# Last layer of a four-layer graph network: its own-quarter blocks in five units of eight block pairs instead of six, and another order of units, products and strip loads

## What is computed

```python
def _L3_gnn_ref(x, adj, weight, bias):
    c = CURV
    deg = jnp.maximum(adj.sum(axis=1, keepdims=True), 1e-08)
    w = adj / deg
    log_ij = _logmap(x[:, None, :], x[None, :, :], c)
    agg = jnp.einsum('ij,ijc->ic', w, log_ij)
    transformed = agg @ weight + bias
    origin = jnp.zeros_like(transformed)
    return _expmap(origin, transformed, c)
...
x = _layernorm(x + _L0_gnn_ref(x, adj, L0_gnn_weight), axis=-1)
x = _layernorm(x + _L1_gnn_ref(x, adj, adj, *L1_weights), axis=-1)
x = _layernorm(x + _L2_gnn_ref(x, adj, L2_gnn_weight, L2_gnn_bias), axis=-1)
x = _layernorm(x + _L3_gnn_ref(x, adj, L3_gnn_weight, L3_gnn_bias), axis=-1)
```

## Time and profile before

| | us |
|---|---|
| Median of 3 runs (1467.49 to 1471.48) | 1470.44 |
| The profiled execution's own time | 1471.95 |
| Its span on the core, first to last instruction | 1470.2 |
| Mean granted TensorE clock of the span | 0.958 |
| Busy over the span: PE / DVE / ACT | 1326.9 / 1204.6 / 982.9 |
| The 72 units' sums (L2888), first to last start | 1051.6 to 1428.7 |

### The profile page before, as it was taken

The page is one execution under the profiler, slowest core; times in us unless marked ns, Lnnn a source line. Parts: engine busy times, 40 slices in busy tenths (PEclk is TensorE's granted clock), DMA queues, the critical chain, the costliest instruction groups (busy, mean ns, idle before and its releaser), DMA issues. The chain is left out here.

```text
span 1470.2 us, 18414 instructions
## 1 busy us (share of the span) xinstructions
PE 1326.9 (90%) x6849; PEld 593.1 (40%) x6874; DVE 1204.6 (82%) x1554; ACT 982.9 (67%) x919; POOL 221.7 (15%) x150
## 2 busy tenths in 40 slices
PE   5899999999898999999999999979987888888893
PEld 1233335334334444444544554434433433334342
DVE  5898978995887888868878977648688898899997
ACT  0001444893673778567676768767789899999985
POOL 1000000000000000000000001242134444444550
PEclk9999999999998999999999999999879999999995
DMA  9999979998999556453554542234533666546610
GB/s 362 409 409 409 374 265 413 409 382 330 415 409 413 185 194 208 178 188 137 191 171 152 193 147 97 90 126 139 205 115 117 213 166 221 184 161 218 219 50 29
DMA packets 134560, 341.56 MB, mean 232 GB/s; under 512 B 7876, under 2 KB 57480, under 8 KB 134280
## 3 DMA queue, kind: packets, MB, share of 16 engines
q1 hardware_dynamic: 118240, 320.88, 59.9%
q10 hardware_dynamic: 16232, 19.51, 3.9%
HBM read 321.49 MB, written 17.83 MB: 231 GB/s over the span
## 5 line engine op out<-in xcount | busy, mean ns | idle before, releaser
L1105 PE MATMUL ps<-ring,X 128*64 128x512 f32 x512 | 235.7, 609 | 7.8 <-DVE ring L2477 7.8
L1106 PE MATMUL ps<-work,X 128*64 128x512 f32 x512 | 235.7, 609 | 0.0
L861 POOL TENSOR_TENSOR ring<-ring,work 128x1024 f32<-128x1024 f32 x72 | 170.1, 2363 | 223.7 <-DVE work L2873 223.7
L1706 ACT ACTIVATE work<-ring 128x2048 f32<-128x2048 f32 x64 | 122.4, 1913 | 89.3 <-PE ps L1121 33.4
L838 POOL TENSOR_SCALAR work<-ring 128x1024 int16<-128x1024 uint8 x24 | 27.4, 1142 | 958.2 <-DMA ring<-codes 884.2
L968 PE MATMUL ps<-ring,work 128*64 128x512 f32 x704 | 160.1, 602 | 1.5 <-DVE Y L2129 1.5
L2477 DVE TENSOR_SCALAR ring<-ring 128x2048 f32<-128x2048 f32 x64 | 78.4, 1225 | 70.4 <-ACT work L1706 70.1
L1105 PEld LDWEIGHTS ps<-ring,X 128*64 128x64 f32 x512 | 67.6, 139 | 146.4 <-issue 139.3
L2151 DVE TENSOR_TENSOR work<-work,ring 128x1024 f32<-128x1024 f32 (+1 forms) x92 | 105.0, 1141 | 4.3 <-DMA ring<-in_adjT 2.4
L1285 PE MATMUL ps<-work 64*128 64x512 f32 x288 | 88.6, 694 | 17.4 <-DVE work L2888 16.0
L1451 ACT ACTIVATE turn_in<-ps 128x512 f32<-128x512 f32 x12 | 7.2, 596 | 144.3 <-PE ps L968 143.4
(11 more groups left out here) (387 smaller groups left out, 2704.0 us busy)
## 6 DMA issues: line engine op xcount, KB each, us to landing
ring<-in_adjT SPq DMA_DIRECT2D x86, 2048.0 KB, 13.6
work<-in_adjT SPq DMA_DIRECT2D x26, 2048.0 KB, 23.1
ring<-in_adjT SPq DMA_DIRECT2D x24, 1024.0 KB, 9.1
ring<-in_adjT SPq DMA_DIRECT2D x48, 512.0 KB, 4.0
ring<-codes SPq DMA_DIRECT2D x32, 512.0 KB, 3.7
ring<-in_adjT SPq DMA_DIRECT2D x64, 256.0 KB, 3.2
codes<-work ACTq DMA_DIRECT2D x32, 256.0 KB, 6.1
codes<-work ACTq DMA_DIRECT2D x64, 128.0 KB, 3.0
```

What stands on the lines that cost most here:

```text
L861: nc.gpsimd.tensor_tensor(u.edges[:, cols], u.edges[:, cols], u.angle[:, cols], ALU.mult).then_inc(weighted, 1)
L1105: nc.tensor.matmul(ps[0:F, h, :], rows, ring[:, r, 2 * (m % 2) + i, cols], start=start, stop=stop)
L1106: mm = nc.tensor.matmul(ps[F:P, h, :], rows, negs[:, m % 2, i, cols], start=start, stop=stop)
L1706: nc.scalar.activation(negs[:, pair], ring[:, r, 2 * pair:2 * pair + 2, :], ACT.Relu, scale=-1.0).then_inc(negs_made, 1)
```

## The change

1. **Five units for a quarter's own pairs.** A new kind **X** (`inner`) takes, in one turned unit, the pairs from blocks 0, 1 to 4, 5 and from 2, 3 to 6, 7. D is now four row blocks against two blocks each, and two of them do for a quarter; the two I stay. Per quarter 2 D + 2 I + 1 X = 5 units (before 4 D + 2 I). In all 48 O, 8 D, 8 I, 4 X = 68 units, of which 60 are turned.
2. **D and X by pieces** (`split`): four edge loads of 256 columns instead of two of 512, four `distances` products of 256 columns instead of two of 512, likewise in `push_apart`. `gather` keeps its four products of 256 columns.
3. **X is a group by itself**: 20 groups instead of 16. Its strip is 0.5 MB (four loads), its sum has 4 sources with one product of 256 columns each, and its `add_mirror` is two operations of 64x256 (a plain copy and one or two memsets where a part has no sum yet).
4. **The planner**: the first group's products go to slots 5 and 6 (before 12 and 13), with a wait for the copied signs, and `turn_sides(2)` now waits for that group's sum. Four sources a slot are also used where a later group would else have to wait (`soon`). Full slots are now 5, 6, 12, 13, 28, 29, 49, 50, 51, 64 and 65; slot 67 has eight sources.
5. **Strips ahead of edges**: the strip's turn stands at `quad_ends[q - 2]`.
6. **The order**: `ORDERS` as in the diff. Groups start at slots 0, 5, 10, 12, 14, 16, 18, 22, 26, 28, 30, 35, 39, 43, 47, 49, 50, 54, 58, 62. In the third string the X stands behind two groups of four O.

```diff
-        ORDERS = [(1, "OOODOODODOODII"), (0, "DDIIDD"), (2, "OOOOOOOODIDIOOOODOOOOD"), (3, "OOOOOOOODIDIOOOOOOOOOOOOOOOODD")]
+        ORDERS = [(1, "OOOODOOOODIIX"), (0, "DIIXD"), (2, "OOOOOOOOXDIIOOOODOOOO"), (3, "OOOOOOOOIIXOOOOOOOOOOOOOOOODD")]
         UNITS = sum(len(order) for I, order in ORDERS)
 
         class Unit:
 
             def __init__(self, n, kind, J, I, k):
                 self.n, self.kind, self.J, self.I = n, kind, J, I
-                self.off, self.turned = kind == "O", kind != "D"
+                self.off, self.turned, self.inner = kind == "O", kind != "D", kind == "X"
+                self.split = kind in "DX"
...
+                elif kind == "X":
+                    self.blocks, self.places = tuple(one[0:2] for one in SETS), (1, 1)
+                    self.seats = (0, GB - 1)
+                    self.sources = [I * CB + c for one in SETS for c in one[2:4]]
                 else:
-                    self.blocks, self.targets = (SETS[0][k], SETS[1][k]), (0, 1)
-                self.rows = tuple(J * CB + b for b in self.blocks)
+                    self.blocks, self.places = tuple((one[k], one[2 + k]) for one in SETS), (0, 1)
+                if not self.split:
+                    self.rows = tuple(J * CB + b for b in self.blocks)
+                self.loads = 1 if self.off else 4 if self.split else 2
...
+            def pieces(self, h):
+
+                return [(b, slice(s * 2 * P, (s + 1) * 2 * P), slice((2 * t + h) * 2 * P, (2 * t + h + 1) * 2 * P))
+                        for s, (b, t) in enumerate(zip(self.blocks[h], self.places))]
...
-            n = max(n, end + (2 if late else 3), LAST_AT + 4)
+            n = max(n, end + (2 if late or not quad else 3), LAST_AT + 4 if quad else 0)
             left = list(range(len(units[end].sources)))
+            soon = quad < 2 or late or n + len(left) // 2 > quad_opens[quad + 2] + 2
             while left:
-                room = len(left) if end == quad_ends[-1] else 4 if quad < 2 or late else 2
+                room = len(left) if end == quad_ends[-1] else 4 if soon else 2
...
-            turns += [(quad_ends[q - 2] + 1, 1, q) for q in range(2, len(quad_ends))]
+            turns += [(quad_ends[q - 2], 1, q) for q in range(2, len(quad_ends))]
...
+                    pe.wait_ge(mirror_added, 1)
...
+                if u.split:
+                    for h in range(2):
+                        for b, at, cols in u.pieces(h):
+                            b += u.J * CB
+                            sp.dma_start(u.edges[:, h * HALF + at.start:h * HALF + at.stop],
+                                         adj_slots[:, b // GB, b % GB, u.I, cols]).then_inc(edges_in[u.row], 16)
+                    return
...
-                    else:
+                    if quad == 0:
+                        pe.wait_ge(signs_copied, SIDED[2])
+                    if quad == 1:
                         wait_for_copies(COPIED[3])
...
+                    h, e = divmod(c, 2)
+                    mine = folded[quad % 2][0][:, h, :].rearrange("p (s e c) -> p s e c", s=2, e=2)[:, :, e, :]
+                    mm = nc.tensor.matmul(ps[0:F, 7, h * 2 * P:(h + 1) * 2 * P].rearrange("p (s c) -> p s c", s=2),
+                                          points[:, u.sources[c], :], mine, start=c == 0, stop=e == 1,
+                                          skip_group_check=True)
+                for t in range(0 if u.inner else 2):
...
+                    V.tensor_tensor(folded[u.quad % 2][0][:, h, :], ps[:, 6 - h, :], strip(u.quad)[:, h, :],
+                                    ALU.mult).then_inc(mirror_weighted, 1)
...
+                    first = 2 * u.J * 2 * P
+                    for part in (2 * u.J, 2 * u.J + 1):
+                        if part not in summed:
+                            V.memset(aggT[F:P, part * 2 * P:(part + 1) * 2 * P], 0.0)
+                    fresh = {2 * u.J, 2 * u.J + 1} - summed
+                    assert len(fresh) != 1 or 2 * u.J in summed
+                    for h in range(2):
+                        sums, bank = aggT[0:F, first + h * 2 * P:first + (h + 1) * 2 * P], ps[0:F, 7, h * 2 * P:(h + 1) * 2 * P]
+                        if 2 * u.J + h in fresh:
+                            ins = V.tensor_copy(sums, bank)
+                        else:
+                            ins = V.tensor_tensor(sums, sums, bank, ALU.add)
+                    summed.update(fresh)
+                    ins.then_inc(mirror_added, 1)
+                    sums_added[1] += 1
```

44 lines of the change are left out of this document (40 added, 4 removed).

## The result

| | before | after |
|---|---|---|
| Median of the runs side by side | 1466.74 us (12 runs, 1463.72 to 1471.48) | 1458.74 us (12 runs, 1453.53 to 1465.29) |
| Ratio, 95% interval | | 0.9942 (0.9929 to 0.9956) |
| Span of the profiled execution | 1470.2 us | 1457.2 us |
| First sum to last sum | 1051.6 to 1428.7: 377.1 us | 1048.6 to 1416.2: 367.6 us |

The change makes the kernel 0.6% faster, 8.0 us between the medians. The forecast was 1460 us. The two figures agree within 1.3 us, and in part by luck: the forecast stood on a median before of 1470.4 us (3 runs) that 12 runs put at 1466.7. As a difference it said -10.6 us, and these runs show -8.0. The changed kernel timed again, on the chip of the last batch, gave 0.9912 (0.9893 to 0.9930), or -11.3 us between the medians. The forecast difference lies between the two.

What follows compares the result with a forecast made beforehand. A plain slot was taken as set by ACT at 4.76 us, DVE right behind. Removing four slots (-19.0 us) less +2.8, +1.3, +2.6, +1.2 and +0.5 gave -10.6 us, from 1470.4 to 1460 us, range 1452 to 1467.

Steps and rivals of the forecast that it cites:

- Four slots: Loop going from 72 to 68 slots: each removed slot gives a plain slot's 4.76 us, -19.0 us in all.
- X turned: The four turned X units: their two more mirror weights each (1.28 us of DVE) hide under ACT, 0.
- Adds: Four more add_mirror: +2.8 us as PE's next group waits, +1.3 us as an X's add is two operations.
- Full slots: Five more slots of sixteen PE passes (11 against 6): 0.52 us each, +2.6 us.
- Norms: Four row norms, two formerly in slots without mirror weights: they lose that cover, 2 x 0.6 = +1.2 us.
- Late strip: Group 16's strip, asked for after slot 49's weighting and used in slot 51, comes late: +0.5 us, range 0 to 4.
- Moves: First group's products moved to slots 5 and 6, and moves behind D units: 0.
- Pieces: Products and loads split into 256 columns: 0, as PE has idle time in a plain slot; bound +3.6 us.
- A: Rival: DVE becomes the bound, a removed slot gives only DVE's time; -4.2 us, 1466 us; chance 0.18.
- B: Rival: two slots removed ahead of slot 20 give 6.25 us each, full slots hide; -16.2 us, 1454 us; chance 0.13.
- C: Rival: handshake gaps on PE drop the clock in 20 more slots, 0.83 us each; +6.0 us, 1476 us; chance 0.05.
- D: Rival: handshakes of groups directly following one another eat the gain, other terms at upper bounds; -0.1 us, 1470 us; chance 0.06.

Runs made afterwards that it cites:

- the first execution: The changed kernel's first profiled execution, nothing edited: 367.6 us from first sum to last, ratio 0.9942 in its set of runs.
- the second execution: The changed kernel profiled once more, nothing edited: 366.5 us from first sum to last, ratio 0.9912 to the kernel before in its set of runs.
- the first experiment: Four of the 72 units, all D, left out of the kernel before, nothing else changed: ratio 0.9865, median 1447.83 us.

## Why the prediction was right, point by point

*Four slots, -19.0 us.* Measured alone: -19.8 (-16.0 to -23.8 by the ratio's interval). Plain slots stayed at 4.80 us.

*X turned, 0.* Right: slot 27 takes 5.20 us with X's mirror weights and 5.19 without. The cover did get thinner, DVE's waits for ACT went from 18.2 to 9.0 us.

*Adds, +2.8 and +1.3.* 0.71 us for one waited-for add was right (0.68, twice). Adds that nobody waits for gave 0.3 us when moved in three slots of five, so they were not free where they stood, and nothing in two, the forecast's lower bound; what the four more adds cost together was not measured by itself. The second of the two terms was too small: the memsets of the X adds, plain in the diff, stood in no term, and they cost 1.25 us in slots 31 and 53.

*Full slots, +2.6.* Mechanism right, size 0.3 to 0.5 us each where it was measured by itself, 0.4 in the mean, instead of 0.52: some +2.1 for five.

*Norms, +1.2.* Over-sized. Seven eighths of all four norms were worth 0.9 us of slots and nothing in the runs. Pricing an operation by its duration was the failing step: it holds only where that engine sets the slot. That PE set the fullest of these slots is what the timeline suggests; no run shows it.

*Late strip, +0.5.* 0, with 0.6 us to spare. The estimates were close: the room was 10.3 us where 9.9 was expected (from the end of slot 49's mirror weights at 1325.54 to 1335.82), and the pair of loads landed 9.6 us after the first was issued, as expected. Undoing the edit cost 4.8 us where 4 was expected.

*Moves, 0.* Right. The scales cost 1.9 us in slot 48 before and after, in spite of the X add that now stands behind them.

*Pieces, 0.* Right, by direct test for `distances`; the four-way split of the edge loads was not tested by itself.

**Sum.** -19.8 for the slots and +7.5 to +8.1 for the X groups make about -12, against -10.6 forecast and -8.0 and -11.3 measured. The small errors have both signs and nearly cancel, which is luck: memsets +1.25 missed; full slots 0.5, norms at least 0.3 and strip 0.5 too high.

*Where the profile should show it.* The first 18 slots were to give 9 to 10 us; they gave 11.3 in the first execution and 9.8 in the second (120.6 - 110.8). The mean from slot 18 on was to be near 5.1 us and was 5.27 and 5.22. Two thirds of the difference in the first execution are the low clock: slots 35 and 36 (2.9 us), 22 and 23 (1.1, against the second execution) and 49 (1.4) make 5.4 us, and (258.3 - 5.4) / 49 = 5.16.

*Rivals.* A (DVE sets every slot) fell by the first experiment: its -13.6 (for the removal alone) lies outside -16.0 to -23.8. B's mechanism, two early slots worth 12.5 us, shows in the kernel without four D (12.2) and less in the changed one (11.3, then 9.8 in the second execution). With the adds first in both kernels the two early slots are worth 7.2 us (118.1 - 110.9). So what they are worth depends on where the low clock falls, and the later stretch takes the rest back: the total is the forecast's. By the rule from the Trainium skill named beside B ("TensorE: Matmul & The Clock Gate", Part 1) a PE that rests less should gain there. The early stretch did go from 0.83 to 0.89, but the later one from 0.99 to 0.96; over the loop the clock was 0.94 before and after, so no run here shows such a gain in the whole from this change. C (20 more slots at the low clock) didn't come. D's waits came (11.2 us of PE waits for adds instead of 5.8), but 1.9 us of them are the scales seen from PE, and D's other terms were not at their bounds.

*What chance adds.* The 13.0 us between the two profiled spans are 9.5 in the loop, 0.5 behind it and 3.0 ahead of the first sum, where the two kernels differ in little but which edge rows are asked for ahead. Over 14 profiled executions the first sum came between 1043.6 and 1051.6 us. A few microseconds between two single profiles mean nothing.
